# Last expert layer: TensorE's blocks as a loop on the engine, and the shared unit's last step after the sorted blocks

## The reference

```python
for j in range(2):                      # layer 0: two rounds, 6 experts, top 2
    weights, ids = top2_softmax(xf @ router_W[j] + ...)
    for e in range(6):                  # unit = up, gate, down, all 256x256
        h = xf @ exp_Wup[e] + exp_bup[e]
        h = silu(h @ exp_Wg[e] + exp_bg[e]) * h
        combined += weights[:, e] * (h @ exp_Wdown[e] + exp_bdown[e])
    s = (xf @ share_Wup + share_bup).reshape(-1, 2, 256)     # two shared units
    s = silu(s @ share_Wg + share_bg) * s
    xf = rmsnorm(xf + combined + (s @ share_Wdown + share_bdown).sum(1))
# layer 1: 8 experts, top 2
    h = gelu(tokens @ W1[e].T + B1[e])                       # 256 -> 512
    acc += c[:, e] * (h @ W2[e].T + B2[e])                   # 512 -> 256
```

## Time and profile before

| | us |
|---|---|
| median of 3 runs | 2036.41 (2035.42 to 2038.35) |
| the profiled execution | 2036.51 |
| its span | 2034.6 |
| PE busy | 1766.5 (87%) |
| DVE busy | 1402.5 (69%) |
| ACT busy | 1029.3 (51%) |
| POOL busy | 821.1 (40%) |

### The profile page before, as it was taken

How to read it: one execution, slowest core, us unless ns; L and a number is a source line. 1 busy time by engine, 2 the same in 40 slices (tenths; PEclk the granted TensorE clock), 3 DMA queues, 4 the chain that set the end, 5 groups by cost and what they waited for, 6 DMA issues and landing times. The chain is left out here.

```text
span 2034.6 us, 31786 instructions
## 1 busy us (share of the span) xinstructions
PE 1766.5 (87%) x11154; PEld 1559.6 (77%) x11154; DVE 1402.5 (69%) x2513; ACT 1029.3 (51%) x2078; POOL 821.1 (40%) x868
## 2 busy tenths in 40 slices
PE   5899999999978999999949999996499883899990
PEld 4788888888877878888838788886266683899990
DVE  4665556546433888777756987775798687688886
ACT  4344334434412344555546355553688353788882
POOL 2132232323211114777721157776221030788840
PEclk8899999999998899999969999998699966899995
DMA  4100000000023131666553226664600013688857
GB/s 155 62 1 11 10 10 0 10 10 0 10 88 103 55 105 40 202 192 202 168 190 122 91 78 199 203 186 146 221 32 1 1 63 114 206 278 277 257 193 258
DMA packets 146216, 231.43 MB, mean 114 GB/s; under 512 B 28082, under 2 KB 103092, under 8 KB 141108
## 3 DMA queue, kind: packets, MB, share of 16 engines
q1 hardware_dynamic: 122484, 165.47, 24.6%
q0 software_dynamic: 23616, 64.52, 10.5%
HBM read 174.07 MB, written 55.33 MB: 113 GB/s over the span
## 5 line engine op out<-in xcount | busy, mean ns | idle before, releaser
L178 POOL TENSOR_TENSOR spare_g<-neg_half 128x1 f32<-128x1 f32 x80 | 20.7, 259 | 622.2 <-ACT a_sg L538 142.5
L167 PE MATMUL bank<-gT_hi,w_hi 128*128 128x512 f32 x592 | 246.0, 416 | 2.4 <-DVE gT_lo L1526 2.4
L167 PE MATMUL bank<-gT_hi,w_lo 128*128 128x512 f32 x592 | 237.3, 401 | 0.0
L167 PE MATMUL bank<-gT_lo,w_hi 128*128 128x512 f32 x592 | 236.2, 399 | 0.0
L1731 POOL DMA_INDIRECT got<-b_rows,b_gather_i x168 | 171.9, 1023 | 65.1 <-issue 50.6
L1526 DVE TENSOR_TENSOR gT_lo<-bank,gT_hi 128x512 fp32r<-128x512 f32 x148 | 97.0, 689 | 132.4 <-ACT gT_hi L1334 99.1
L1364 ACT ACTIVATE m_hi<-gs 128x512 fp32r<-128x512 f32 x116 | 73.0, 633 | 128.3 <-DVE gs L1533 69.0
L167 PEld LDWEIGHTS bank<-gT_hi,w_lo 128*128 128x128 f32 x592 | 113.2, 191 | 27.6
L167 PE MATMUL bank<-w_hi,m_hi 128*128 128x256 f32 x464 | 130.5, 281 | 2.8 <-DVE shared L1555 1.4
L167 PEld LDWEIGHTS bank<-gT_hi,w_hi 128*128 128x128 f32 x592 | 113.6, 192 | 22.9 <-DVE gT_lo L1526 2.5
L167 PEld LDWEIGHTS bank<-gT_lo,w_hi 128*128 128x128 f32 x592 | 113.9, 192 | 21.5
(11 more groups left out here) (455 smaller groups left out, 5731.2 us busy)
## 6 DMA issues: line engine op xcount, KB each, us to landing
v_raw<-in_units SPq DMA_DIRECT2D x39, 1024.0 KB, 5.0
w_raw<-in_units SPq DMA_DIRECT2D x52, 256.0 KB, 4.9
shared<-in_units SPq DMA_DIRECT2D x40, 256.0 KB, 4.4
b_rows<-x SPq DMA_DIRECT2D x16, 512.0 KB, 2.9
got<-b_rows SPq DMA_DIRECT2D x16, 512.0 KB, 3.9
close_back<-b_kept SPq DMA_DIRECT2D x16, 512.0 KB, 7.8
d_back<-d_kept SPq DMA_DIRECT2D x16, 512.0 KB, 8.5
w_raw<-b_folded SPq DMA_DIRECT2D x24, 256.0 KB
```

Of the source, the lines that this page charges most:

```text
L167: ins = pe.matmul(out, a, b, start=first and n == 0, stop=last and n == of - 1)
L178: eng.tensor_tensor(b.spare_g[:, i:i + 1], b.neg_half[:, 0:1], b.neg_half[:, 0:1], ALU.mult)
```

## The change

1. **Stage D.** TensorE's blocks 2 to 25 become a loop on the engine of two iterations with twelve blocks in a body; blocks 0, 1 and 26 to 38 stay written out. The ring of gathered rows keeps its six buffers, which get a name (`GOTS`). TensorE's program gets about 500 rows shorter.
2. **A round's order.** With `LATE = 1`, the "old" step of tile 7 moves from ahead of the 21 sorted steps to behind them. It needs the shared unit's weights once more (`LATE_LOAD`), and its row tile again (SP loads it into a slot of the ring of gathered rows, `row_slot`). The first gathers wait for a turn one step earlier. The loop over sorted steps starts one step earlier.
3. **Places.** The three buffers that the fetched results of round 0 use are taken in another order (`b.back`), and `close_back` and `x_old` move in SBUF. After round 1 SP waits for the last result of the late step behind the first fetch.

```diff
+GOTS, UNROLL = 6, 12
+LATE = 1
+FRONT_STEPS, LATE_LOAD = 2 * NB - LATE, 2 + NBB
-STEPS, LB, WM = 2 * NB + NBB, 2 + NBB, KD * D
+STEPS, LB, WM = 2 * NB + NBB, 3 + NBB, KD * D
...
-        order = [("new", t) for t in range(NB)] + [("old", t) for t in range(NB)] + [("sort", k) for k in range(NBB)]
+        order = [("new", t) for t in range(NB)] + [("old", t) for t in range(NB - LATE)]
+        order += [("sort", k) for k in range(NBB)] + [("old", t) for t in range(NB - LATE, NB)]
...
+    for t in range(NB - LATE, NB):
+        sp.wait_ge(r.gT_ps.sem, r.gT_ps.at(first_sort(rnd * NBB + NBB - 4 + t - (NB - LATE))))
+        sp.dma_start(b.got[:, row_slot(t, rnd), :, :], rows_of(dram.rows[rnd], t)).then_inc(r.reloaded[t % 4].sem, 16)
...
-    first, rounds = 2 * NB, (NBB - 2) // TURNS
+    first, rounds = FRONT_STEPS, (NBB - 2) // TURNS
...
-            g.wait_ge(r.gT_ps.sem, r.gT_ps.at(rnd * STEPS + 2 * NB - 1))
+            g.wait_ge(r.gT_ps.sem, r.gT_ps.at(rnd * STEPS + FRONT_STEPS - 1))
...
     old_rows(0)
+    sp.wait_ge(r.o.sem, r.o.at(2 * OUTS - 1))
...
-    for k in range(NBD):
-        if k + 1 < NBD:
-            up(k + 1)
-        if k + 2 < NBD:
-            turn(k + 2)
-        down(k)
+    step(0)
+    step(1)
+    rounds = (NBD - 4) // UNROLL
+    with pe.Fori(0, rounds) as q:
+        for u in range(2, 2 + UNROLL):
+            step(u, q)
+    for u in range(2 + rounds * UNROLL, NBD):
+        step(u)
...
-                b.back = [b.got[:, 2 * i:2 * i + 2, :, :] for i in range(2)] + [b.sent_both]
+                b.back = [b.sent_both, b.got[:, 2:4, :, :], b.got[:, 0:2, :, :]]
```

More of the change, by code:

```diff
@@ L37 @@
 CLOSE_BUFS = 4
+GOTS, UNROLL = 6, 12
+C_GAP = 5168
 TURN_COLS = 8
@@ L1006, in __init__ @@
         self.rnd, self.first, self.count = rnd, rnd * STEPS, STEPS
-        order = [("new", t) for t in range(NB)] + [("old", t) for t in range(NB)] + [("sort", k) for k in range(NBB)]
+        order = [("new", t) for t in range(NB)] + [("old", t) for t in range(NB - LATE)]
+        order += [("sort", k) for k in range(NBB)] + [("old", t) for t in range(NB - LATE, NB)]
         self.steps, users = [], {}
         for j, (kind, n) in enumerate(order):
-            load = {"new": 0, "old": 1}.get(kind, 2 + n)
+            load = {"new": 0, "old": 1 if j < FRONT_STEPS else LATE_LOAD}.get(kind, 2 + n)
             i = self.first + j
@@ L1016, in at, with row_slot @@
         return self.steps[j] if 0 <= j < self.count else None
+def row_slot(t, rnd):
+    return t % 4 if t < NB - LATE else (rnd * NBB + NBB + t - (NB - LATE)) % 4
 def turn_steps(rnd):
@@ L1100, in b_sync @@
         sp.wait_ge(r.fold_kept.sem, r.fold_kept.at(0))
-    for t in range(NB):
+    for t in range(NB - LATE):
         if t >= 4:
@@ L1316, in rounded @@
         elif st.load >= 2:
-            act.wait_ge(done.sem, done.at(rnd * (OUTS if done is r.down_ps else STEPS) - 1))
+            ended = LATE if st.load % LB == 0 else 0
+            act.wait_ge(done.sem, done.at(rnd * (OUTS if done is r.down_ps else STEPS) - 1 - ended))
         act.activation(b.w_hi_flat[st.load % 2][:, lo:hi], b.w_raw[i][:, lo:hi], ACT.Copy).then_inc(sig.sem, 1)
@@ L2400, in d_gpsimd @@
     g.wait_ge(r.gather_at.sem, r.gather_at.at(0))
-    for n in range(AHEAD):
+    for n in range(GOTS):
         gathers(n)
@@ L2404, in d_gpsimd @@
     for n in range(NGD):
-        if n + AHEAD < NGD:
-            gathers(n + AHEAD)
+        if n + GOTS < NGD:
+            gathers(n + GOTS)
         for k in range(GROUP * n, min(GROUP * (n + 1), NBD)):
@@ L2441, in up @@
         for o in range(KH):
-            if k >= 2 and o % 2 == 0:
+            if u >= 2 and o % 2 == 0:
                 pe.wait_ge(r.m_lo.sem, r.m_lo.at(k - 2, o // 2 + 1))
@@ L2446, in up, with down @@
                 ins.then_inc(r.up_ps.sem, 1)
-    def down(k):
-        par, down_bank = k % 2, d_banks(b, k)[1]
+    def down(u, q=None):
+        k, par, down_bank = u if q is None else q * UNROLL + u, u % 2, d_banks(b, u)[1]
         pe.wait_ge(r.m_lo.sem, r.m_lo.at(k))
         pe.wait_ge(r.w2_lo.sem, r.w2_lo.at(k))
-        if k >= 2:
+        if u >= 2:
             pe.wait_ge(r.o.sem, r.o.at(k - 2))
@@ L2457, in down, with step @@
         ins.then_inc(r.down_ps.sem, 1)
+    def step(u, q=None):
+        if u + 1 < NBD:
+            up(u + 1, q)
+        if u + 2 < NBD:
+            turn(u + 2, q)
+        down(u, q)
     turn(0)
@@ L2745, in program @@
             b.c_y, b.c_e, b.c_l, b.c_t = (sb(sc, n, [P, 2 * KD, TB]) for n in ("c_y", "c_e", "c_l", "c_t"))
+            b.x_old = [sb(sc, f"x_old{t}", [P, CT, D]) for t in range(1, CLOSE_BUFS)]
+            b.c_gap = sb(sc, "c_gap", [P, C_GAP])
+            b.x_old.insert(0, sb(sc, "x_old0", [P, CT, D]))
+            b.close_back = [sb(sc, f"close_back{t}", [P, PICKS, CT, D]) for t in range(CLOSE_BUFS)]
             bC = Names(b)
@@ L2758, in program @@
             with ExitStack() as e:
-                b.got = [sb(e, f"d_got{i}", [P, GROUP * QBD, D]) for i in range(6)]
+                b.got = [sb(e, f"d_got{i}", [P, GROUP * QBD, D]) for i in range(GOTS)]
                 b.gT_hi, b.gT_lo = ([sb(e, f"d_{n}{i}", [P, KD, BSD], F32R) for i in range(2)] for n in ("gT_hi", "gT_lo"))
@@ L2891, in program @@
         rd.fetched = [rb.closing[i].again(1, 16 * PICKS) for i in range(4)] + [s.load_c[i].again(1, 16 * PICKS) for i in range(4)]
-        rd.gathered = [rb.gathered[i].again(uses_of(2 * NBB, 4, i), 16 * GROUP * QBD) for i in range(4)] + [signal(f"d_gathered{i}", 16 * GROUP * QBD) for i in range(4, 6)]
+        rd.gathered = [rb.gathered[i].again(uses_of(2 * NBB, 4, i), 16 * GROUP * QBD) for i in range(4)] + [signal(f"d_gathered{i}", 16 * GROUP * QBD) for i in range(4, GOTS)]
         rd.scattered = [rb.scattered[i].again(uses_of(2 * NBB, SENDS, i), 16 * QBD) for i in range(4)]
```

41 lines of the change are left out of this document (22 added, 19 removed).

## The result

The changed kernel is slower: 1.0071 times the time before, 95% interval 1.0047 to 1.0095. Applied to the median before, 2036.4 us, that is 2050.9 us. Its four executions took 2048.6 to 2058.4 us (median 2052.5). The profiled one took 2048.58 us, 12.1 more than the profiled one of before.

What follows compares the result with a forecast made beforehand. POOL's chain was taken to bound layer 0's expert rounds and TensorE stage D. Round ends of 4.7 and 4.0 us plus 1.9 for the loop made 10.6 us on 2036.5: 2047.1 us, range 2040 to 2052.

Steps and rivals of the forecast that it cites:

- What bounds the kernel: POOL's descriptor chain bounds layer 0's expert rounds; TensorE bounds stage D, where each `up` head's wait has no slack.
- The start of the sorted blocks: First gather 0.36 us earlier, TensorE idle about 8.2 us; sorted steps at +0.65 us in round 0, +0.1 in round 1.
- rival D: Faster: gathers start a step earlier, last scatters 5.1 us earlier in both rounds; 2028.2 us, chance 0.10.
- The loss of clock: After standing still ahead of the sorted steps, TensorE runs at low clock: 1.6 us lost, 2.7 kept for the range.
- The end of the round: Late step's work delays sorted block 20's send, so last scatters start later: +4.0 us in round 0, +4.7 in round 1.
- Rival C: No change: block 20's send at the rounds' ends is not held up as thought; 2039 us, chance 0.14.
- What else moves costs nothing that I can find.: Late step's own down and send, SP's new wait, extra loads and swapped buffers were claimed hidden or free: no cost.
- Stage D's loop: In 24 looped blocks the `d_gT_lo` wait moves to a register instruction, 0.08 us each: +1.9 us, bounds nothing to +3.8.
- The back edge (rival B): Stage D's branch back stalls TensorE on instruction fetch: 4.4 to 8.7 us on top, 2051.5 to 2055.8 us; chance 0.12.
- The sum: Both round ends and stage D together: 4.7 + 4.0 + 1.9 = 10.6 us slower, giving 2047.1 us.

Runs made afterwards that it cites:

- the filled stillstand: Changed kernel with stage D written out, plus 56 unread transposes on TensorE while it waits for a round's first gathers; 1.0018 times the kernel before.
- the early turn: Kernel before, with each stage D block's turn and its halves one place earlier on three engines; 0.9979 times the kernel before, without or with the loop.

## Why the prediction was right, and where its sizes were off

**What bounds the kernel.** Right, for both places. POOL's chain decided the end of the rounds and gave way to PE when block 20 came late; in stage D the head of each `up` was on the path, and what was added to it came out in full.

**The start of the sorted blocks.** Right in kind: no step is gained, PE stands still for 8.40 and 8.22 us (8.2 forecast), and rival D fell because the index is ready no earlier. The gather followed the index by 0.30 us, not by the 0.81 that I took, so counted from the round's first turn the first gathers start 0.8 us (round 0) and 1.0 us (round 1, without the 0.8 named below) earlier, not the 0.36 forecast. The loss of clock was forecast as 1.6 us, and the filled stillstand measures 2.2 and 1.9, between the two rows that I had (1.5 and 2.7). It agrees with the granted clock: 0.50 for 4.9 and 3.8 us with PE busy throughout loses half of that, 2.4 and 1.9. The window that I read at 1137 was 3 us long and gave a lower bound, not a price. Nor is the row at 1136.69 a fixed price of its stillstand of 2.58 us: over the twelve traces the eight transposes behind it took 1.09 to 1.97 us, while behind the stillstand of over 8 us they took 1.94 in all five kernels that have it.

**The end of the round.** The order on DVE and PE holds block 20 back as worked out. In round 0 the scatters start 4.56 us later, of which 0.5 came into the round with it: 4.1 against the 4.0 forecast. That so little is left between the two is in part luck: the first sorted turn came 0.5 us earlier than worked out and the clock cost 0.6 us more. In round 1 the stage is 3.5 longer, 4.7 were forecast. Of this difference 0.8 lies ahead of the sorted blocks: from the round's first turn to the turn at 1136.69 it was 91.7 us before and 90.9 after (1049.59 to 1140.48). This length varies from trace to trace, 91.0 to 91.7 in the kernels without the late step and 90.3 to 91.6 in those with it; no run isolates it. The rest (0.4) is for the most part the earlier gather: the fourth started 0.7 us earlier, not 0.36. Putting block 20's work first on both engines removed POOL's wait, on DVE alone it did not, since TensorE's `down` then arrives late as well. Rival C falls with POOL's wait of 4.83 us for block 20 in both rounds.

**"What else moves costs nothing that I can find."** True for the changed kernel, and only by the cover that the late scatters give: with them mended, SP's queue holds round 0's fetch for 1.8 us behind the weights' load, and in round 1 its new wait on the late step's last result stands for 5.1 us behind the first fetch. I had named that second wait as one that the late scatters cover, and so it is in the changed kernel. Of the first I had looked at the extra loads' own use, not at what stands behind them in the queue.

**Stage D's loop.** The step that was mis-sized. "24 x 0.08 = +1.9 us" took from the earlier trace rows the price of one instruction behind the release (by the source two waits stand ahead of that transpose, the one on `a_v` first, so one instruction stands between it and the transpose); stage D's `up` has two instructions behind it, and each costs: 0.16 a block, 3.9 us. The stage as a whole is 4.4 longer; the other 0.5 is within the 1 us by which this stage varies between traces. This was the upper bound named (3.8). The order rows show the two instructions, so the count could have been made before.

**The back edge (rival B).** Did not come. Body of about 1330 instructions or not, the block with the branch back takes 6.48 us like its neighbours. The stall that the Trainium skill, "Runtime: NRT & Kernel Launch", "Instruction fetch mechanics", has behind a taken branch out of the fetched window is not seen in these traces. Whether it was hidden or not there, they don't show, nor whether this branch leaves that window.

**The sum.** 10.6 us were forecast. The traces have 7.6 in the rounds (8.7 forecast) and 4.4 in stage D (1.9 forecast), 12.0 together and 12.1 in the profiled executions as a whole; the timed ratio has 14.5, interval 9.6 to 19.3. That the sum is as near as it is owes something to luck: it had the rounds 1.1 us too high and stage D 2.5 too low.

## What to carry to other kernels

In TensorE's loop here, all waits but the last ahead of a matmul stand on instructions of their own, and each such instruction between the release and the matmul adds 0.07 to 0.1 us where the wait is exposed. Put the wait that really ends last on the work itself, by writing it last, or better, make what it waits for ready earlier: then the loop was free. A step that is moved behind others takes its instructions on every engine with it: look for the one result that the end waits for, and put it ahead on all engines, then look at what stands ahead of the fetch in the DMA queue, and at every wait in it for a result that now comes last. A cover can hide such a cost: the length of a stage "as before" can be a gain and a loss that cancel, so compare its parts.

## What the runs showed that I had not expected

The execution-to-execution spread of all these kernels is larger than first seen, and a part of it is TensorE's clock in layer 1's attention, which no edit touches. Windows of its first 48 us, the kernel before, then the loop alone (PEclk is the third number from the end):

```profile
1447.00:1495.00 48.00, 37.68 (x127) 23.35 (x127) 42.92 (x86) 40.27 (x77) 13.31 (x18) 0.82 0.31 102
```

```profile
1447.00:1495.00 48.00, 37.96 (x117) 23.10 (x118) 41.18 (x82) 37.62 (x73) 11.06 (x17) 0.74 0.34 108
```

With a mean clock of 0.74 in place of 0.82 this stage took 187.1 us in the second trace and 183.9 in the first, 3.1 us from nothing that was changed: nearly as much as stage D's loop. Two more traces have 186.9 us, both of kernels with the loop and without the late step; the fourth kernel of that kind has 183.3, and all others 182.9 to 185.1. That it goes with the execution and not with the loop is seen from the early turn: its traces without and with the loop have 183.2 and 186.9 us in this stage, yet both kernels were timed at 0.9979. What sets the clock so in one execution and not in another is open. Comparing whole profiled executions would have put that on the change; cutting the traces into stages did not.
